# A four-layer graph stack on one core: last layer's weights prepared inside the first units, eps folded into the aggregation, other orders

## The reference

```python
h = jnp.maximum(_layernorm(x, axis=-1), 0.0)          # eps = 1e-5 under the root
x = x + _L0_gnn_ref(h, adj, L0_gnn_W, L0_gnn_a)       # attention: leaky_relu(s1 + s2), mask adj > 0, softmax
h = jnp.maximum(_layernorm(x, axis=-1), 0.0)
x = x + _L1_gnn_ref(h, adj, a0, a1, a2, a3)           # scores (h * a_r) h^T by edge type, softmax, times h
h = jnp.maximum(_layernorm(x, axis=-1), 0.0)
x = x + _L2_gnn_ref(h, L2_gnn_adj, adj, weight, bias) # per edge type: mask, gather, weight; sum and bias
h = jnp.maximum(_layernorm(x, axis=-1), 0.0)
x = x + _L3_gnn_ref(h, adj, L3_gnn_W, L3_gnn_a)       # attention as layer 0, then elu
```

## Time and profile before

| | |
|---|---|
| median of 3 runs | 299.83 us |
| the profiled execution, its own time | 299.55 us |
| its span, first to last instruction | 297.7 us |
| PE matmuls busy | 279.9 us (94%) |
| DVE busy | 261.3 us (88%) |
| ACT busy | 260.2 us (87%) |
| POOL busy | 224.8 us (76%) |
| mean granted TensorE clock | 0.994 |

### The profile page before, as it was taken

How to read it: one execution, slowest core, us unless ns; L and a number is a source line. 1 busy time by engine, 2 the same in 40 slices (tenths; PEclk the granted TensorE clock), 3 DMA queues, 4 the chain that set the end, 5 groups by cost and what they waited for, 6 DMA issues and landing times.

```text
span 297.7 us, 8186 instructions
## 1 busy us (share of the span) xinstructions
PE 279.9 (94%) x2250; PEld 259.4 (87%) x2250; DVE 261.3 (88%) x1355; ACT 260.2 (87%) x849; POOL 224.8 (76%) x363
## 2 busy tenths in 40 slices
PE   1899999999998999999999999999999899999992
PEld 1799998888987999998888999998888799999991
DVE  2689999888888898999999999988888889799995
ACT  3799997799999985899999889799999998589993
POOL 4987777676776999987768787777677699997800
PEclk9999999999999999999999999999999999999997
DMA  6925555310000000011111660000000000001223
GB/s 185 356 72 160 166 166 148 116 47 0 2 1 2 0 3 1 3 36 55 53 57 53 191 204 1 3 1 2 0 3 0 3 1 0 2 3 36 74 72 107
DMA packets 15949, 17.77 MB, mean 60 GB/s; under 512 B 2720, under 2 KB 11808, under 8 KB 15904
## 3 DMA queue, kind: packets, MB, share of 16 engines
q1 hardware_dynamic: 15072, 17.11, 18.2%
q10 hardware_dynamic: 832, 0.13, 0.3%
HBM read 13.05 MB, written 4.19 MB: 58 GB/s over the span
## 4 chain that ended last, share of the span: by engine, by line
PE 67%; DVE 20%; ACT 6%; issue 3%; DMA 1%; ACTq 0%; DVEq 0%
PE bank L929 19%; PE bank L875 9%; PE bank L880 9%; DVE pT L644 6%; PE bank L851 6%; PE bank L823 5%; PE bank L914 5%; PE bank L900 4%; DVE result L687 4%; DVE st L574 3%; PE bank L926 3%; PE bank L888 2%; PE bank L882 2%; PE bank L838 2%; DVE expy L678 2%
## 5 line engine op out<-in xcount | busy, mean ns | idle before, releaser
L346 POOL TENSOR_TENSOR rs<-ve,minus_half 128x2 f32<-128x2 f32 x128 | 89.9, 702 | 53.7 <-DVE ve L588 51.9
L929 PE MATMUL bank<-val,pT 128*128 128x129 f32 x512 | 74.7, 275 | 0.0
L929 PEld LDWEIGHTS bank<-val,pT 128*128 128x128 f32 x512 | 67.9, 193 | 0.0
L360 POOL TENSOR_TENSOR h<-h,rs 128x256 f32<-128x256 f32 x96 | 59.8, 623 | 0.1
L644 DVE SCALAR_TENSOR_TENSOR pT<-bank,val,edgesT 128x256 f32<-128x256 f32 x128 | 55.8, 478 | 3.7 <-PE bank L888 3.4
L574 DVE BATCH_NORM_STATS2 st<-x 128x6 f32<-128x128 f32 x192 | 44.3, 272 | 0.0
L851 PE MATMUL bank<-w_gat,hT 128*128 128x131 f32 x256 | 42.2, 288 | 0.3 <-ACT hT L447 0.2
L354 POOL TENSOR_TENSOR h<-x,mv 128x256 f32<-128x256 f32 x64 | 39.9, 623 | 2.5
L479 ACT ACTIVATE val<-bank,val 128x128 f32<-128x128 f32 x128 | 41.3, 391 | 0.0
L926 PE MATMUL bank<-ident,vsum 128*128 128x128 f32 x128 | 35.5, 278 | 3.3 <-DVE x L670 1.0
L823 PE MATMUL bank<-ident,h 128*128 128x128 f32 x192 | 38.5, 283 | 0.0
(11 more groups left out here) (80 smaller groups left out, 664.8 us busy)
## 6 DMA issues: line engine op xcount, KB each, us to landing
edges<-in_adj SPq DMA_DIRECT2D x32, 256.0 KB, 3.5
xin<-in_x SPq DMA_DIRECT2D x32, 128.0 KB, 2.7
out_x<-result SPq DMA_DIRECT2D x32, 128.0 KB, 1.7
w_rel<-in_L_gnn_weight SPq DMA_DIRECT2D x1, 256.0 KB, 3.5
w_gat<-in_L_gnn_W ACTq DMA_DIRECT2D x2, 64.0 KB, 3.4
a_rel<-in_L_gnn_a SPq DMA_DIRECT2D x4, 0.5 KB, 4.3
bias<-in_L_gnn_bias SPq DMA_DIRECT2D x1, 64.0 KB, 3.6
a_gat<-in_L_gnn_a ACTq DMA_DIRECT2D x2, 1.0 KB, 3.5
```

Source lines behind the costliest of these rows:

```text
L346: pool.tensor_tensor(rs[:, g % WIDE], ve[:, g % WIDE], minus_half[:, :], ALU.pow).then_inc(rs_ready, 1)
L360: pool.tensor_tensor(h[:, n % HS, :, 0:D], h[:, n % HS, :, 0:D], rs[:, g % WIDE, :].rearrange("p (t o) -> p t o", o=1).to_broadcast([P, T, ...
L929: last = pe.matmul(bank_o(n)[:, t], pT[:, n % 4, u, t * P:(t + 1) * P], values[:, u], start=(u == 0 and layer == 1), stop=(u == T - 1), sk ...
```

## The change

1. `LAG_MAX` goes from 14 to 13 and `SP_LAG` from 8 to 10.
2. `add_eps`, its tile `ve` and its semaphore are gone. `st` has nine columns per row in place of six; POOL fills the third triple once at the start (0, 0, D * EPS), `bn_stats` writes the first six, and `bn_aggr` reads all nine, so that the variance it gives contains eps. POOL's power reads the variance out of `mv`.
3. Only layer 0's weights are prepared ahead of the first unit. Layer 3's are loaded on SP's queue behind the second graph's edges, and prepared inside units 4, 6 and 7 of layer 0, in unused columns of the bank of `put_hT`. The range check reads a copy (`norm_sums`) and runs inside `check_weights`.
4. The lists of all four engines have other lags and another order.

```diff
-        st = sb("st", [P, WIDE, T, 6])
+        st = sb("st", [P, WIDE, T, 9])
-        ve = sb("ve", [P, WIDE, T])
...
+                if k == 2:
+                    sp.dma_start(w_gat[1][:, 0:D], w3).then_inc(gat_loaded[1], 16)
+                    sp.dma_start(a_gat[1][:, :], a3.rearrange("(c p) o -> p (c o)", c=2), allow_slow_non_contiguous=True).then_inc(gat_loaded[1], 16)
...
+            pool.memset(st[:, :, :, 6:8], 0.0).then_inc(ident_ready, 1)
+            pool.memset(st[:, :, :, 8:9], D * EPS).then_inc(ident_ready, 1)
...
-                pool.wait_ge(ve_ready, nth(ALL, n))
-                pool.tensor_tensor(rs[:, g % WIDE], ve[:, g % WIDE], minus_half[:, :], ALU.pow).then_inc(rs_ready, 1)
+                pool.wait_ge(mv_ready, nth(ALL, n))
+                pool.tensor_tensor(rs[:, g % WIDE], mv[:, g % WIDE, :, 1], minus_half[:, :], ALU.pow).then_inc(rs_ready, 1)
...
             def take_hT(n, layer, g):
                 k = g % SLOTS
                 act.wait_ge(hT_put, nth(ATTEND, n))
+                if ORDER[n] == (0, 4):
+
+                    scale_a(1)
+                    take_wT(1, bank[HT_BANK[n]])
+                if ORDER[n] == (0, 6):
+
+                    take_wa(1, bank[HT_BANK[n]])
+                if ORDER[n] == (0, 7):
+
+                    act.wait_ge(norms_put, 1)
+                    act.activation(norm_sums[:, :], bank[HT_BANK[n]][0:1, 500:504], ACT.Copy).then_inc(norms_taken, 1)
...
-            def add_eps(n, layer, g):
-                k = g % SLOTS
-                dve.wait_ge(mv_ready, nth(ALL, n))
-                dve.tensor_scalar(ve[:, g % WIDE], mv[:, g % WIDE, :, 1], EPS, None, ALU.add).then_inc(ve_ready, 1)
...
-            pipeline([(mean_and_variance, 2, LAST), (statistics, 1, LAST), (add_x, 14, LAST),
...
+            pipeline([(mean_and_variance, 1, LAST), (rectify, 3, MULTI_REL), (statistics, 0, LAST),
...
+                if ORDER[n] == (0, 4):
+
+                    put_wT(1, bank[HT_BANK[n]])
+                if ORDER[n] == (0, 6):
+
+                    put_wa(1, bank[HT_BANK[n]])
```

More of the change, by code:

```diff
@@ L371, in add_bias @@
                                    ALU.add).then_inc(xb_ready, 1)
[L373 to L378, removed]
+            pipeline([(add_bias, 3, RGCN_REL), (inverse_deviation, 2, LAST), (inverse_deviation, 2, FIRST),
+                      (scale_deviation, 3, FIRST), (scale_deviation, 3, MULTI_REL),
+                      (inverse_deviation, 2, MULTI_REL), (subtract_mean, 2, MULTI_REL),
+                      (scale_deviation, 3, LAST), (inverse_deviation, 2, RGCN_REL),
+                      (subtract_mean, 2, LAST), (subtract_mean, 2, FIRST)])
             pool.wait_ge(flag_ready, 1)
@@ L410, in softmax_steps, with scale_a @@
                 act.activation(gpT[:, :, :], ps_p, ACT.Copy).then_inc(g_step, 1)
[L413 to L416, removed]
+            act.dma_start(w_gat[0][:, 0:D], w0).then_inc(gat_loaded[0], 16)
+            act.dma_start(a_gat[0][:, :], a0.rearrange("(c p) o -> p (c o)", c=2), allow_slow_non_contiguous=True).then_inc(gat_loaded[0], 16)
+            act.wait_ge(ident_ready, 9)
             act.activation(junk[:, 0:1], ones[:, :], ACT.Exp)
-            for i in range(2):
+            def scale_a(i):
                 act.wait_ge(gat_loaded[i], GAT_WEIGHTS)
@@ L423, in _, with take_wT, take_wa @@
                 act.activation(a_four[i][:, 3:4], a_gat[i][:, 1:2], ACT.Copy, scale=SLOPE).then_inc(a_scaled, 1)
+            def take_wT(i, b):
                 act.wait_ge(wT_done, i + 1)
-                act.activation(w_gatT[i][:, :], ps_w[i][:, 0:D], ACT.Copy).then_inc(wT_ready, 1)
-            for i in range(2):
+                act.activation(w_gatT[i][:, :], b[:, 256:256 + D], ACT.Copy).then_inc(wT_ready, 1)
+            def take_wa(i, b):
                 act.wait_ge(wa_done, i + 1)
[L428 to L431, removed]
+                act.activation(w_gat[i][:, D:D + 4], b[:, 500:504], ACT.Copy).then_inc(constants, 1)
+                act.activation(norms[:, 2 * i:2 * i + 2], b[:, 500:502], ACT.Square).then_inc(norms_ready, 1)
+            scale_a(0)
+            take_wT(0, ps_w)
+            take_wa(0, ps_w)
             def normalize(n, layer, g):
@@ L688, in add_x @@
                                          ALU.add).then_inc(result_ready, 1)
[L690 to L698 removed]
+            pipeline([(mean_and_variance, 1, LAST), (rectify, 3, MULTI_REL), (statistics, 0, LAST),
+                      (residual, 10, RGCN_REL), (take_z, 8, MULTI_REL), (invert_sums, 10, FIRST),
+                      (invert_sums, 10, LAST), (invert_sums, 10, MULTI_REL), (minus_mean, 3, RGCN_REL),
+                      (mean_and_variance, 1, RGCN_REL), (residual, 10, MULTI_REL), (take_rows, 8, FIRST),
+                      (elu, 12, LAST), (residual, 10, FIRST), (take_rows, 8, LAST), (add_x, 13, LAST),
+                      (mean_and_variance, 1, FIRST), (statistics, 0, MULTI_REL), (statistics, 0, FIRST),
+                      (statistics, 0, RGCN_REL), (mean_and_variance, 1, MULTI_REL)])
             dve.wait_ge(scores_taken, COUNTS[MULTI_REL][-1])
@@ L795, in turn, with put_wT, put_wa @@
                 pe.wait_ge(g_step, g * G + AT[name])
-            pe.wait_ge(ident_ready, 7)
-            for i in range(2):
+            pe.wait_ge(ident_ready, 9)
+            def put_wT(i, b):
                 pe.wait_ge(gat_loaded[i], GAT_WEIGHTS)
-                pe.transpose(ps_w[i][:, 0:D], w_gat[i][:, 0:D], ident[:, :]).then_inc(wT_done, 1)
-            for i in range(2):
+                pe.transpose(b[:, 256:256 + D], w_gat[i][:, 0:D], ident[:, :]).then_inc(wT_done, 1)
+            def put_wa(i, b):
                 pe.wait_ge(wT_ready, i + 1)
                 pe.wait_ge(a_scaled, i + 1)
-                pe.matmul(ps_w[i][:, 256:260], w_gatT[i][:, :], a_four[i][:, :], start=True,
-                          stop=True).then_inc(wa_done, 1)
-            pe.wait_ge(constants, 2)
-            pe.wait_ge(norms_ready, 1)
-            pe.matmul(ps_w[0][0:1, 264:268], ones[:, :], norms[:, :], start=True, stop=True).then_inc(norms_put, 1)
+                pe.matmul(b[:, 500:504], w_gatT[i][:, :], a_four[i][:, :], start=True, stop=True).then_inc(wa_done, 1)
+            put_wT(0, ps_w)
+            put_wa(0, ps_w)
             def put_hT(n, layer, g):
@@ L824, in put_hT @@
                 last.then_inc(hT_put, 1)
+                if ORDER[n] == (0, 4):
+                    put_wT(1, bank[HT_BANK[n]])
+                if ORDER[n] == (0, 6):
+                    put_wa(1, bank[HT_BANK[n]])
+                if ORDER[n] == (0, 7):
+                    pe.wait_ge(norms_ready, 2)
+                    pe.matmul(bank[HT_BANK[n]][0:1, 500:504], ones[:, :], norms[:, :], start=True,
+                              stop=True).then_inc(norms_put, 1)
             def put_edgesT(n, layer, g):
```

52 lines of the change are left out of this document (24 added, 28 removed).

## The result

The changed kernel takes **301.67 us** (median of 8 runs, 300.78 to 303.45) against 299.82 (8 runs, 299.61 to 300.18) before: ratio 1.0069, 95% interval 1.0042 to 1.0095. It is slower by 0.7%, where 298.2 was forecast, and outside the range (295.6 to 299.9). The profiled execution took 300.78 us with a span of 298.9 (before 299.55 and 297.7).

A forecast was written before the change was run, and what follows sets the result against it. PE was taken to bound layers 0 and 1, DVE and ACT the way from layer 3 to layer 0. Terms -1.1 + 0.5 - 1.0 + 0 = -1.6 us on 299.55 gave 297.95, as median 298.2 us; range 295.6 to 299.9.

The forecast's parts named there:

- layer 3 and the way to layer 0: First pass: removing `add_eps` and blocks offsets each result's 0.25 us loss to POOL; net 0, ends -1.2 and +1.5 us.
- the three blocked `add_eps`: Between 119 and 154 us: three `add_eps` stalled by POOL cost DVE 1.7 of 4.0 us of blocks before.
- The second layer 3: Second pass of layer 3: only three such steps before the statistics end, and DVE not behind; 0.
- the port decides, slower than before: Layer 3 to layer 0: result and `elu` both run into POOL, step 2.94 us, up to 304 us; chance 0.08.
- The remark that the fold costs no `bn_aggr` time: Rival on the aggregation: a third triple might cost `bn_aggr` time; no measurable price; no chance given.
- The start: First units: PE starts 1.8 us earlier, idles 0.8, clock rise stays near 14 us; gain 1.1 us, ends 0.5 and 3.2.
- Where layer 0 turns into layer 1: `residual(13)` moves ahead of `take_z` and the check, so PE's 0.84 us wait goes; -1.0 us.
- The moved weights: Layer 3's transpose and product, with the sum of squares, move into a full stage of layer 0; PE pays +0.5 us.

The follow-up runs named there:

- 299.08: The kernel before with only the fold (eps in the aggregation), and POOL's subtraction and scaling of layer 3 on 8 of 128 columns: 299.08 us, ratio 0.9970.
- 298.96: The kernel before with POOL's subtraction and scaling of layer 3 on 8 of 128 columns: 298.96 us, ratio 0.9979.
- 0.9993: The kernel before with only the last layer's weight preparation placed as in the change: 299.44 us, ratio 0.9993.
- POOL small in layer 3: The changed kernel with POOL's subtraction and scaling of layer 3 on 8 of 128 columns: 294.10 us, ratio 0.9817.
- 302.85: The changed kernel with POOL's power, in layer 3 and the ten units behind it, also waiting for DVE's reciprocal of the same step: 302.85 us, ratio 1.0097.
- 301.11: The changed kernel with the result directly behind `elu`, both ahead of `take_rows`, and POOL's power held for the reciprocal: 301.11 us, ratio 1.0051.
- 300.97: The changed kernel with the result directly behind `elu`, and POOL's scaling held for the result of the unit 11 back: 300.97 us, ratio 1.0047.
- the kernel of 294.80 us: The changed kernel with the result directly behind `elu`, and POOL's scaling held for the result of the unit 10 back: 294.80 us, ratio 0.9854.

## Why the prediction was wrong

**The step that failed** is layer 3 and the way to layer 0: "POOL's power is now released by the step's first instruction, 0.32 into it", so that the subtraction begins 1.65 into every step, "POOL blocks until 0.51 of its 0.61", and "each result loses 0.25". Three things in it were wrong.
- *The release.* I took POOL to be waiting for DVE. It was not: earlier release only gave it more backlog, 5.0 us at 124.03, and it ran back to back until 133.75. In before it had caught up at 123.55, ahead of the first result (129.26 us), which is why before looked mild. The offset was set by POOL's own cycle, not by DVE's.
- *The length of a block.* The 0.51 holds for the second operation, but scaling and subtraction follow each other without a gap, and DVE did not get in between: 1.26 us for 0.41, a loss of 0.85 and not 0.25, when it began inside the scaling. The evidence stood in the rows I had read: `add_eps` took 1.01 at 122.46, through both operations. I quoted it as a single case.
- *The lock.* Two catches of 0.85 and a free step of 2.24 make 3.94, which is two POOL cycles of 1.97, so the offset reproduces itself. I had summed blocks one by one.

Where POOL does wait for DVE, the same working came out. On the way to layer 0 six results from 139.80 to 151.99 take 0.61 or 0.62 us (forecast 0.65), the step is 2.44 (forecast 2.45 to 2.5), and four times from 154.13 on `elu` takes 0.83 or 0.84 (forecast a loss of 0.4):

```profile
139.53 0.61 POOL L359 TENSOR_TENSOR h<-xin,mv 128x256 f32<-128x256 f32 x1
139.80 0.62 DVE L703 SCALAR_TENSOR_TENSOR result<-expy,x 128x256 f32<-128x256 f32 x1
```

So what failed is the premise that POOL waits, in the part of layer 3 where it does not. A smaller slip is in the sum: of the three blocked `add_eps` (1.7 us) the trace between 119 and 154 us has two, 1.1 us.

The term was 0 with ends of -1.2 and +1.5. Measured are some 3 us from layer 3 to the end of layer 0. **The second layer 3**, which I had at 0, lost 2.7. The reason I gave ("DVE is not behind there") doesn't bear on a lock that makes its own delay.

**The rival** "the port decides, slower than before", given 0.08, was nearest to the mechanism. It had ten steps at 2.94 in place of two at 3.94, with milder ones around them, so its mechanism is the port but not the lock. Its price, 4.5 us in the first pass and 1.3 in the second, comes to about the measured 3 and 2.7 in sum; as neither part is right, that is luck. Its argument "against", that the offset is late in POOL's operation, rested on the same wrong release. The remark that the fold costs no `bn_aggr` time was right (168 ns in the mean, and 299.08 against 298.96 with the port out of the way); that it therefore has no price was not.

**The start** was right in place and too small in size. The timeline after, as the earlier trace rows:

```profile
4.06 0.71 POOL L351 TENSOR_TENSOR rs<-mv,minus_half 128x2 f32<-128x2 f32 x1 [1.88 <-DVE mv L604]
...
6.74 0.69 PE L837 MATMUL bank<-ident,h 128*128 128x128 f32 x2 [1.18 <-POOL h L365]
...
8.62 0.66 PE L837 MATMUL bank<-ident,h 128*128 128x128 f32 x2 [0.77 <-POOL h L365]
...
9.07 1.08 PE L879 MATMUL bank<-w_gat,hT 128*128 128x131 f32 x4
...
11.74 0.71 PE L879 MATMUL bank<-w_gat,hT 128*128 128x131 f32 x4
```

Power at 4.06 (forecast 4.1), `put_hT` at 6.74 (6.9), idle 0.77 (0.8). But `put_v` is near full speed from 11.74 on, where it should have been at half until about 14: the rise came some 2 us earlier, with PE's start. (The profile's granted clock reads 1.00 from the first microsecond on in both kernels, so the speed is read from the durations here.) Start and weights together were to bring 0.6 us by layer 1 and brought 1.85 in this trace. The nine kernels that have the change's start reach the first score product between 46.17 and 47.16 us, before at 48.04, so it is 0.9 to 1.9. I cited the Trainium skill, "TensorE: Matmul & The Clock Gate", on transposes, that they don't count as work for the clock, by which the rise would not move. It did move; but `put_v` also began earlier (9.07 against 9.89), and no run separates the two, so this case does not decide on the rule.

**Where layer 0 turns into layer 1** I gave -1.0. The wait of 0.84 us is gone, and another stands in its place:

```profile
54.63 0.63 PE L928 MATMUL bank<-ident,prob 128*128 128x128 f32 x4 [0.73 <-ACT prob L521]
```

From its first unit's score product to its last unit's, layer 1 gained 0.26 us. Layer 2, where I had nothing moved, gained 0.8; I did not take that apart. **The moved weights** at +0.5 were not seen in the runs (0.9993), against a start 0.4 us earlier in the same kernel. With POOL small in layer 3 the change gains 4.9 us where the sum has 1.6, so the forecast was too low on the gain as well as blind to the loss; the runs don't split those 4.9 us further.

## What to carry to other kernels

When an edit releases an engine earlier, ask first whether that engine is waiting there at all: if not, the edit adds to its backlog, and moves the moment from which the others set its phase. Two engines that block each other through a port should be read as two cycles with an offset, and the longest block in the trace of before is a forecast, not an outlier. A cheap remedy is a wait on the blocking operation for an event behind the victims. Here it was worth 3.6 us by itself and 6.9 with the two victims put side by side. It has to bind: the three kernels whose hold was met already, or but for once in each half (302.85, 301.11 and 300.97 us), gained little or nothing.

## What the runs showed of the hardware

- A DVE instruction with two SBUF inputs (`elu`, 128x256) that started 0.2 us into a POOL `tensor_tensor` of 0.61 us was held through that one and the adjacent next: 1.26 us for 0.41. One that started 0.27 us into the second took 0.62 (139.80). It got on about 0.1 us before the end of the second (0.40 before its own end at 128.12 is 127.72, and the subtraction ended at 127.83). The Trainium skill, "SBUF — State Buffer", on who interferes with whom, says that the port is held for the whole instruction; here it was two instructions less 0.1 us. `add_eps`, which reads one SBUF tensor, was held in the same way (1.01 us at 122.46).
- One that started late in the power (0.42 us into the one of 124.00), and was not done when the scaling began, was held for longer: the result of 124.42 in the kernel of 294.80 us took 1.70.

```profile
124.42 1.70 DVE L705 SCALAR_TENSOR_TENSOR result<-expy,x 128x256 f32<-128x256 f32 x1
124.66 0.61 POOL L367 TENSOR_TENSOR h<-h,rs 128x256 f32<-128x256 f32 x1
125.23 0.61 POOL L359 TENSOR_TENSOR h<-x,mv 128x256 f32<-128x256 f32 x1
```

- The power itself (128x2) did not hold DVE: an `elu` at 134.36, beside the power of 134.29 and done before the scaling of 134.94, took 0.41. The power took longer, 0.86 for 0.69, where it started while an `elu` or a result was running (127.80).
- DVE instructions that read PSUM (`take_rows`) and `bn_stats` ran at their free duration beside POOL's large operations in the timelines shown.
